# Three small-head attention layers: a pair-by-pair schedule rewritten as a stream of score banks

## What is computed

```python
# layer 1: 16 heads of 16, 256 keys (context), key mask
scores = einsum('bhqd,bhkd->bhqk', q, k) * scale;  attn = softmax(where(mask, scores, min))
hidden = einsum('bhqk,bhkd->bhqd', attn, v) @ cproj_w + cproj_b + residual;  x = hidden + MLP(ln(hidden))
# layer 2: 16 heads of 16, 512 keys (256 of the context, 256 of the tokens), key mask
attn = softmax(where(full_mask, einsum('bkhd,bnhd->bhkn', q, kmat) / DH, -inf))
x = MLP(rmsnorm(attn @ v @ out_w + out_b + residual)) + residual
# layer 3: 32 query heads on 8 key/value heads of 8, 256 keys, full additive mask
attn = softmax(einsum('bkgld,bksd->bkgls', q, k) * scale + mask);  out = layernorm(attn @ v @ Wo + bo + x)
```

## Time and profile before

| what | value |
|---|---|
| time before, median of 3 runs | 1412.97 us (1408.93 to 1414.95) |
| profiled execution, its own time | 1412.02 us |
| its span in the profile | 1410.7 us |
| layer 1 (first score to last `OS` copy) | about 719 to 849 us |
| layer 2, the same | about 916 to 1119 us |
| layer 3 | about 1183 us to the end |
| mean granted TensorE clock | 0.93 of full speed |

### The profile page before, as it was taken

The page is one execution under the profiler, slowest core; times in us unless marked ns, Lnnn a source line. Parts: engine busy times, 40 slices in busy tenths (PEclk is TensorE's granted clock), DMA queues, the critical chain, the costliest instruction groups (busy, mean ns, idle before and its releaser), DMA issues. The chain is left out here.

```text
span 1410.7 us, 26853 instructions
## 1 busy us (share of the span) xinstructions
PE 1289.9 (91%) x9901; PEld 1098.9 (78%) x9901; DVE 903.1 (64%) x2341; ACT 721.6 (51%) x1817; POOL 547.4 (39%) x1003
## 2 busy tenths in 40 slices
PE   7999999999999999998977787978888898999995
PEld 6999999999999999997865556855554587666663
DVE  6866767688856767687765657455556375465661
ACT  4866666677756666576214443235444522444442
POOL 3544544445444545453443325043323131223332
PEclk9999999999999999999986889968997798899997
DMA  5320000023200000022012101220120112011000
GB/s 166 105 69 1 2 1 5 2 68 112 62 2 1 2 1 1 1 71 92 24 47 72 48 2 46 69 77 25 50 70 1 50 42 79 17 37 56 13 3 16
DMA packets 44132, 56.69 MB, mean 40 GB/s; under 512 B 10016, under 2 KB 24416, under 8 KB 44000
## 3 DMA queue, kind: packets, MB, share of 16 engines
q1 hardware_dynamic: 38880, 54.40, 12.3%
q0 software_dynamic: 5120, 0.56, 0.3%
HBM read 32.68 MB, written 1.05 MB: 24 GB/s over the span
## 5 line engine op out<-in xcount | busy, mean ns | idle before, releaser
L1797 ACT ACTIVATE PT<-bank 128x512 f32<-128x512 f32 x320 | 174.2, 595 | 165.5 <-PE bank L1739 84.2
L1078 POOL TENSOR_SCALAR E<-E,rl 128x256 f32<-128x256 f32 x256 | 238.1, 941 | 0.0
L1903 POOL DMA_DIRECT2D Q<-rows x160 | 90.3, 566 | 216.4 <-ACT rows L1811 208.5
L1076 POOL TENSOR_TENSOR pb<-E,rl 128x2 f32<-128x2 f32 x128 | 33.7, 263 | 327.4 <-DVE rl L954 327.4
L821 ACT ACTIVATE QTh<-bank,bqs 128x256 fp32r<-128x256 f32 x128 | 60.7, 474 | 182.6 <-PE bank L117 182.6
L1861 DVE CUSTOM_DVE_ANT_0 Em<-bank,M 128x256 bf16<-128x256 f32 x256 | 95.2, 420 | 75.7 <-issue 45.5
L1854 DVE TENSOR_REDUCE nm<-bank 128x1 f32<-128x512 f32 x128 | 82.3, 685 | 74.2 <-PE bank L1708 73.7
L831 ACT ACTIVATE E<-bank,nm 128x257 f32<-128x257 f32 x256 | 119.3, 480 | 3.1 <-DVE nm L931 3.1
L938 DVE SCALAR_TENSOR_TENSOR QTl<-bank,bqs,QTh 128x256 fp32r<-128x256 f32 x128 | 61.8, 483 | 85.3 <-ACT KT L822 84.4
L1754 PE MATMUL bank<-PT,V 128*32 128x256 f32 x1280 | 103.7, 462 | 2.6 <-ACT PT L1797 2.6
L1731 PE MATMUL bank<-Q,K 51*128 51x256 f32 (+1 forms) x640 | 97.4, 319 | 6.3 <-ACT PT L1797 5.4
(11 more groups left out here) (465 smaller groups left out, 4505.5 us busy)
## 6 DMA issues: line engine op xcount, KB each, us to landing
stage<-in_wts SPq DMA_DIRECT2D x99, 256.0 KB, 3.1
Q<-stage SPq DMA_DIRECT2D x72, 128.0 KB
K<-stage SPq DMA_DIRECT2D x48, 128.0 KB
K<-xh SPq DMA_DIRECT2D x16, 128.0 KB, 2.9
Q<-rows POOLq DMA_DIRECT2D x96, 4.0 KB, 1.7
K<-stage SPq DMA_DIRECT2D x24, 64.0 KB
X<-in_x SPq DMA_DIRECT2D x4, 256.0 KB, 6.0
stage<-in_ctx SPq DMA_DIRECT2D x4, 256.0 KB, 3.6
```

What stands on the lines that cost most here:

```text
L1078: m = pool.tensor_scalar(s.E[:, i % 3, t, 0:256], s.E[:, i % 3, t, 0:256], s.rl[:, r, t:t + 1], None, ALU.mult)
L1797: act.activation(s.PT[i % s.NPT][:, 2 * u:2 * u + 2, :].rearrange("p a b -> p (a b)"), s.STB[y][:], ACT.Exp).then_inc(S["t_ex"])
L1903: pool.dma_start(f32(s.Q[b % s.NR][at:at + 2, pair:pair + n, :]), f32(s.rows[4 * n * y:4 * n * y + 4 * n, g % 2, :])).then_inc(S[f"dma_row ...
```

## The change

In layers 1 and 2 a step is now made of score *banks*. `WIDTH` says how many banks a step handles: 1 in layer 1 (one head), 2 in layers 2 and 3 (a unit of a pair in layer 2, a whole pair in layer 3, as before). Every batch has 16 steps in every layer. `LAG` replaces `DELAY` (13 steps of half a pair, 7 steps of half a pair's work, 5 pairs), `TURN` and `MEET` say how many steps behind the maxima are turned and the values come, and `KEPT` gives layer 1 eight `PT` buffers in place of six. In layer 1 values are made in two pieces in successive steps (8 instructions each), in layer 2 too (16 each). Each projection is split into two halves of six matmuls with names of their own (`k0`, `k1`; `q0`, `q1`; `v0`, `v1`; `x0`, `x1` for the tokens' keys, `v2`, `v3` for their values; `c0`, `c1`), its ACT part (`kh`), its DVE part (`kl`) and its DMAs (`k_out`) are placed one by one. In layer 2 PE issues the second score bank of a step after the scores by key and the values. In every layer PE does the finishing of the last batch ahead of the preparation of the next. `prep_bank_free` follows a list of who held the bank last (`HELD`). No engine computes anything else than before.

```diff
-DELAY = {1: 6, 2: 4, 3: 5}
+WIDTH = {1: 1, 2: 2, 3: 2}
+LAG = {1: 13, 2: 7, 3: 5}
+TURN = {1: 3, 2: 1, 3: 1}
+MEET = {1: (2, 2), 2: (1, 2), 3: (1, 1)}
+KEPT = {1: 8, 2: 6, 3: 6}
...
-IN_LAYER = {1: {0: ["mask", "k", "stats"], 1: ["v0", "k_out", "norm", "maskrow"], 2: ["turn", "scale"],
-                3: ["parts", "mask_out"], 4: ["q"], 5: ["q_out"]},
...
+IN_LAYER = {1: {0: ["mask", "k0", "stats"], 1: ["k1", "kh"], 2: ["kl", "norm"], 3: ["k_out", "maskrow"],
+                4: ["turn", "scale", "mask_out"], 5: ["v0", "th"], 6: ["v1", "va", "tl"], 8: ["q0"], 9: ["q1", "qh"],
+                10: ["ql"], 11: ["q_out"]},
+            2: {0: ["mask", "turn", "th", "tl"], 2: ["q0", "maskrow"], 3: ["q1", "qh", "ql"], 5: ["k0"],
+                6: ["k1", "kh", "kl", "mask_out"], 7: ["q_out", "k_out"], 8: ["x0"], 9: ["x1", "xh", "xl"],
+                10: ["x_out"], 12: ["v0", "v1", "va"], 14: ["v2", "v3", "vb"]},
...
+POSTS = {1: [["po0", "on0"], ["po1", "on1"], ["onT", "oth"], ["otl"], ["c0"], ["c1", "y"]],
+         2: [["po0", "on0"], ["po1", "on1"], ["onT", "oth", "otl"], [], ["c0"], ["c1", "y"]],
...
+    def turns_at(self, n):
+
+        g, r = divmod(n - TURN[self.l] + 1, self.G * self.units // self.WD)
+        return [g - 1] if r == 0 and 0 < g <= 2 * self.N // self.G else []
+
+    def attends_at(self, n):
+
+        off, parts = MEET[self.l]
+        g, k = divmod(n - self.L - off + 1, self.four)
+        m = self.nkt // parts
+        return [(g - 1, m * k + e) for e in range(m)] if 0 < g <= self.N // 2 and k < parts else []
...
+    def by_key(n, e):
+
+        p, u, y = s.unit(n)
+        q, r, g = p % s.P, p // s.P % s.NR, 2 * p // s.G
+        at, o = slice(64 * y, 64 * y + s.R + 2), (2 * u + e) * 128
+        w.wait_ge(S[f"dma_rows{g % 2}"], 32 * ((s.o["g"] + g) // 2 + 1))
+        w.wait_ge(S["t_ex"], s.o["ex"] + n - 1)
...
-    for p in range(s.steps()):
-        for u in range(s.units):
-            if p < s.N:
-                scores(p, u)
-            if 0 <= p - s.D < s.N:
-                weights_by_key(p - s.D, u)
-        for g in s.turns_at(p):
+    for n in range(s.steps()):
+        queries(n, 0)
+        if l == 3:
+            queries(n, 1)
+        keys(n - s.L)
+        for g in s.turns_at(n):
             turn_maxima(g)
-        for gi in s.attends_at(p):
-            attend(gi)
-        b, steps = s.preps(p)
+        for gi, k in s.attends_at(n):
+            attend(gi, k)
+        if l == 2:
+            queries(n, 1)
+        b, steps = s.posts_at(n)
+        for x in steps:
+            heads_post_pe(c, s, b, x)
+        b, steps = s.preps(n)
         for x in steps:
             heads_prep_pe(c, s, b, x)
```

More of the change, by code:

```diff
@@ L1143 @@
+POSTS_MLP = [["po0", "on0"], ["po1", "on1"], ["onT", "oth", "otl"], ["c0", "c1", "y"]]
+NEXT_NORMS = {0: [(0, "stats")], 1: [(0, "norm")], 3: [(0, "turn"), (0, "scale")], 5: [(0, "parts")],
+              7: [(1, "stats")], 8: [(1, "norm")], 10: [(1, "turn"), (1, "scale")], 12: [(1, "parts")]}
 class Heads:
@@ L1465, in tokens_free @@
                 w.wait_ge(S["pe_v1"], b)
-    if x == "parts" and l == 1:
+    if x == "th" and l == 1:
         w.wait_ge(S["h_hf"], b + 1)
@@ L1742, in attend, with by_query @@
-    def attend(gi):
+    def by_query(n):
+        p, u, y = s.unit(n)
+        q, r = p % s.P, p // s.P % s.NR
+        at = slice(64 * y, 64 * y + s.R)
+        w.wait_ge(S["t_mx"], s.o["mx"] + (n - 1) * (2 if l == 3 else 1))
+        if l == 2:
+            pe.matmul(s.SB[y][:], s.Q[r][at, q, u * 128:u * 128 + 128], s.K[r][at, q, :], start=True, stop=True
+                      ).then_inc(S["t_s"])
+            return
+        for e in range(2):
+            z = pe.matmul(s.SB[y][:, 256 * e:256 * e + 256], s.Q[r][at, q, 128 * e:128 * e + 128],
+                          s.K[r][at, q // s.rp, :], start=True, stop=True)
+        z.then_inc(S["t_s"])
@@ new lines, in by_key @@
+    def by_key(n, e):
+        p, u, y = s.unit(n)
+        q, r, g = p % s.P, p // s.P % s.NR, 2 * p // s.G
+        at, o = slice(64 * y, 64 * y + s.R + 2), (2 * u + e) * 128
+        w.wait_ge(S[f"dma_rows{g % 2}"], 32 * ((s.o["g"] + g) // 2 + 1))
+        w.wait_ge(S["t_ex"], s.o["ex"] + n - 1)
+        if n < 2:
+            w.wait_ge(S["m_x"], 4 * (l - 1) + 2)
+        z = pe.matmul(s.STB[y][:, 256 * e:256 * e + 256], s.K[r][at, q // s.rp, o:o + 128], s.Q[r][at, q, :],
+                      start=l != 3 or e == 0, stop=l != 3, skip_group_check=l == 3)
+        if l != 3 and e == 1:
+            z.then_inc(S["t_st"])
@@ new lines, in add_mask, with queries @@
+    def add_mask(n):
+        b, bank = n // (s.WD * s.TB), s.STB[n % 2]
+        w.wait_ge(S["mask_low"], b + 1)
+        w.wait_ge(S["ident_r"], 1)
+        pe.matmul(bank[:], s.identR[:], s.MTh[:, b % 2, :], start=False, stop=False, skip_group_check=True)
+        pe.matmul(bank[:], s.identR[:], s.MTl[:, b % 2, :], start=False, stop=True, skip_group_check=True
+                  ).then_inc(S["t_st"])
+    def queries(n, y):
+        if y == 0 and n < s.T and n % s.TB == 0:
+            ready(n // s.TB)
+        if y == 0 and n < 2:
+            w.wait_ge(S["m_gelu"], 16 * l)
+        for k in s.in_step(n)[y:y + 1]:
+            by_query(k)
@@ L1743, in attend, with keys @@
+    def keys(n):
+        if l == 3:
+            for e in range(2):
+                for k in s.in_step(n):
+                    by_key(k, e)
+            for k in s.in_step(n):
+                add_mask(k)
+        else:
+            for k in s.in_step(n):
+                by_key(k, 0)
+                by_key(k, 1)
+    def attend(gi, k):
         b, g = gi // (nh // 4), gi % (nh // 4)
@@ L1751, in attend @@
             w.wait_ge(S["m_x"], 4 * (l - 1) + 3)
[L1752 to L1756 removed]
+        for q in range(4):
+            z = pe.matmul(s.OB[32 * q:32 * q + 32, 0:256], s.V[b % s.NV][:, k, (4 * g + q) // s.rep, :],
+                          s.PT[(i0 + q) % s.NPT][:, k, :], start=k == 0, stop=k == nkt - 1, skip_group_check=True)
+        if k == nkt - 1:
+            z.then_inc(S["t_pv"])
     def turn_maxima(g):
```

351 lines of the change are left out of this document (153 added, 198 removed), and 2 rows, old and new, of the table IN_LAYER.

## The result

The change makes the kernel slower: 1448.42 us median (1440.87 to 1458.27, 4 runs) against 1413.2 of before (1408.93 to 1414.95, 4 runs), a ratio of 1.0245 with a 95% interval of 1.0212 to 1.0278. Forecast were 1376 us and 1350 to 1408. Each ratio is against the kernel before as it ran beside that kernel (medians of 1412.87 to 1415.7 us), and isn't the quotient of the two medians.

A forecast was written before the change was run, and what follows sets the result against it. Layers 1 and 2 were taken as bound by PE and DVE stopping each other in turn. Gains of 25 us in layer 2 and 10.4 in layer 1, off 1412.0, gave 1376.4 us; range 1350 to 1408.

The forecast's parts named there:

- the share of half clock: Layers 1 and 2: PE at half clock 20% and 8% of the time, against 42 and 40% before.
- The rival that ends on the other side: Layers 1 and 2: clock falls and stays down, PE bounds at half speed; 35 us slower, 1447 us; chance 10%.
- The wait added at the turn: Layer 2: PE waits at turned maxima one step after their last bank; 1.5 us a batch, bounds 0 and 5.2.
- The late DMAs of q: Layer 1, head of next batch: q's low part arrives 0.5 to 1 us late a batch; 0.8 us taken.
- The step sum without clock and turn: Layers 1 and 2: larger of PE and DVE per step at full clock; 22.7 and 36.0 us a batch before additions.
- changes of tile shape: Layer 2 on PE: some 22 more changes between scores, values and projections a batch; 1.8 us, 1.0 counted.
- Reading of the bound: Layers 1 and 2: no engine is full; PE and DVE stop each other in turn, a loss of order.
- the 1.10 us of two scores "apart": Layer 2 on PE: two scores take 1.10 us apart, against 0.51 us standing together.
- Filling and draining: Start and end of layers: left alone in the sum; 18.8 of layer 2's 202.8 us before the change.
- Layer 3: Layer 3: keeps its pairs and order of scores, PE already full; 0, give or take 3 us.
- "Wrong" signs: PE waiting over 5 us for POOL or Q's DMAs; layer 1 pairing lost; clock 0.8 or less with PE full.

The follow-up runs named there:

- the eight rows of the table: Layer 2 in profiled executions of the kernel before, the changed kernel and six reorderings of its scores, values and turned maxima: lengths from 185.6 to 243.0 us.
- the run with S1 ahead of T: Changed kernel, but in layer 2 a step's second score stands directly behind the scores by key, before turned maxima and values: 1394.94 us, ratio 0.9877.
- the run with V ahead of T: Changed kernel, but in layer 2 the values stand before the turned maxima, the second score still last: 1410.25 us, ratio 0.9971.

## Why the prediction was wrong

**The step that failed: the share of half clock.** I took 8% of the time in layer 2 and 20% in layer 1. By the granted clock it was 70% and 68% (0.65 and 0.66 in the windows), above the 44 and 47% from which I had said that it decides. The rival that ends on the other side, given 10%, is what happened: at half clock PE is the bound, busy 94 and 96% of two long stretches. Its 1447 us hit the 1448 partly by luck: for 70% it had 11 and 24 us, where layer 1 lost 9.7 and layer 2 40, and some 10 us came back later. The argument for my share, that scores, projections and values come close together, was an argument from what PE does, and the traces contradict it: cutting blocks finer neither kept the clock up nor kept it down by itself. What went with the clock in layer 2 was how often the engines stop each other: over the eight rows of the table (and whole blocks, 0.73 with 86.8 us) the clock falls almost in step with the waits of DVE for its banks. A slower PE also lengthens those waits, so that is no proof of the direction. The order edits, which change no instruction, prove that the order sets both; whether the clock fell by the waits stays open, and so does what kept it down. In layer 1 the cause of the low clock is open too: of its two edits, the sooner turn changed nothing and the sooner q helped in two of three executions.

**The wait added at the turn** was the second error. What it waits for and what is queued behind it were right, and so was the upper bound of 5.2 us a batch; I took 1.5, because even steps seemed PE's, and 4.8 were measured. That the wait feeds itself (the second score behind the turn makes the next maximum late, and that the next turn) is argued, not shown: the halved wait in the run with S1 ahead of T is for it, and the run with V ahead of T, which kept S1 last and won 38 us, is against it as the whole reason. What the early turn costs at full clock is 2.0 us in the four steps that can be compared with the turn later (11.8 less 9.8).

**The late DMAs of q.** The term was 0.8 us a batch; the full-clock batches give 24.4 less 23.7, 0.7 us. One stall was 2.34 us, though, longer than the 0.5 to 1 that I had, and the clock fell behind it. With the sooner q layer 1 took 125 us in two profiled executions and 134 in a third, where the clock fell all the same.

**The step sum without clock and turn** was good. Layer 1: 24.4 us measured, 23.5 forecast. Layer 2: 36.0 and 1.0 make 37.0 without the turn; 40.2 measured with the turn later. The 3 us are probably changes of tile shape: I counted 1.0 for 22 of them. From a score to a projection the lone score shows 0.2 us (0.42 in place of 0.22), from a projection to a score it is 0.09 (1036.31 to 1036.52, in place of 0.12). By these two prices 22 changes are 2.0 to 4.4 us, an estimate that holds the 3 us; no run measured them apart. The page TensorEngine Tiling (Array Packing) of the Trainium skill (Key Properties) says that a change of tiling mode drains TensorE. This trace agrees, with 0.09 and 0.2 us at full clock, where I took 0.08 from the earlier trace rows. With the share of half clock put in, the sum for layer 1 holds (90% of the time at half: 23.5 / (1 - 0.90 x 0.33) = 33.4, measured 32.5); for layer 2 it is 9 us low (66%: 38.5 / (1 - 0.66 x 0.37) = 50.9, measured 60.2). The waits at the turn and the shapes are the likely rest.

**Reading of the bound.** That layers 1 and 2 lose by order held, and finer steps do win: whole blocks cost 25 us more than halves in the same loop. The version with scores together, the turn a step later and q sooner is 31 us faster than before, against the 36 us that I forecast; about 7 of the 31 are layer 3's, which I had at nothing. One reading of the earlier trace rows was wrong, though it entered no term: the 1.10 us of two scores "apart" hold a wait, as the second starts 0.60 us behind the first, when DVE has freed its bank.

**Last batch of layer 1.** Not in the sum at all. Filling and draining I left alone, but the last batch, with no preparation beside it, took 24.9 us at a clock of 0.50, where it took 18.2 at 0.89 before. With filler at a clock near 1.00 it took 15.5.

**Layer 3** was forecast at 0, give or take 3. It wins about 7 us, at its start and by the clock.

**"Wrong" signs.** Two of the signs that I named came: PE waits for POOL at the turn by far more than 5 us, and the clock is at 0.8 or less with PE full. The third, scores and products of y = 0 and y = 1 no longer side by side in layer 1, didn't: at 798.39 and 798.40 they start together.

## What to carry to other kernels

When an instruction moves next to a wait, ask first what stands behind it in that engine's queue and whether the engine that it waits for needs one of those. Price such a wait at its upper bound (here 4.8 us a batch of 5.2 possible, where I took 1.5). Put the producer of the next wait (here the second score) ahead of the wait, or let the wait come a step later: the first won 54 us here and the second 36, and each is a change of a line or two. And where a layer already spends 40% of its time at half clock, small waits are not priced by their length: here 9 us of idle time came with 49 us of slower matmuls, so try the orders on the chip before trusting a sum at full clock.

## What the runs showed of the hardware

TensorE stayed at its lower level, 1.2 GHz, for 44 and 31 us on end while it was busy 94 and 96% of the time, with four waits of PE of 0.36 to 0.89 us in the longer of the two; it had fallen behind 6.9 us at full clock with PE busy for 5.2 and a wait of 1.06 us at the turn. With two added matmuls of 128 rows ahead of each score bank, the same program held 0.84 in place of 0.65. The page TensorE: Matmul & The Clock Gate of the Trainium skill (A second HAM failure mode: psum-queue depth-cycling) tells of brief idling between groups of matmuls as the cause of a clock that oscillates. This trace agrees for the fall, and no run here shows it for the staying down. What brings the clock back is open: whole blocks were tried and did not (0.73, against 0.80 with halves).

The clock also varies between executions of like code: layer 1's third batch in the banks' order, with q sooner, had 0.89, 0.89 and 0.56 in three profiled executions, each of another kernel with the same layer 1. So single batches at less than full clock say little, and the runs of one kernel spread over 5 us (the one with the turn later and scores together) to 21 us (q sooner alone).
